# A transformer block on one core: head groups paired in one PSUM bank, merged causal masks, fewer waits, and a written list for each engine

## What is computed

```python
h = _layernorm(x) * (1 + ca) + sa
q, k, v = (split_heads(h @ W + b) for W, b in ((Wq, bq), (Wk, bk), (Wv, bv)))
att = softmax(where(causal, einsum('bhtd,bhsd->bhts', q, k) / sqrt(8), -inf))
y = einsum('bhts,bhsd->bhtd', att, v).transpose(...).reshape(B, T, 128) @ Wo + bo
x = x + ga * (layernorm(y) * gamma + beta)
h = _layernorm(x) * (1 + cb) + sb
x = x + gb * (sum over the top 2 experts of coef * ((silu(h @ gate) * (h @ up)) @ down)
              + (silu(h @ shared_gate) * (h @ shared_up)) @ shared_down)
```

## Time and profile before

| | us |
|---|---|
| Median of 3 runs (551.6 to 552.94) | 552.45 |
| The profiled execution | 553.16 |
| its span on the core | 551.4 |
| PE busy in the span | 502.8 (91%) |
| DVE, ACT, POOL busy | 359.7, 292.2, 254.1 |
| prologue, first turn | 0 to 24.9, 24.9 to 78.4 |
| middle turns | 78.4 to 446.9 |
| final turn, tail | 446.9 to 505.5, 505.5 to 551.4 |

### The profile page before, as it was taken

The page is one execution under the profiler, slowest core; times in us unless marked ns, Lnnn a source line. Parts: engine busy times, 40 slices in busy tenths (PEclk is TensorE's granted clock), DMA queues, the critical chain, the costliest instruction groups (busy, mean ns, idle before and its releaser), DMA issues.

```text
span 551.4 us, 10280 instructions
## 1 busy us (share of the span) xinstructions
PE 502.8 (91%) x3626; PEld 273.1 (50%) x3626; DVE 359.7 (65%) x806; ACT 292.2 (53%) x615; POOL 254.1 (46%) x366
## 2 busy tenths in 40 slices
...
DMA packets 35795, 37.93 MB, mean 69 GB/s; under 512 B 8832, under 2 KB 30880, under 8 KB 35616
## 3 DMA queue, kind: packets, MB, share of 16 engines
...
## 4 chain that ended last, share of the span: by engine, by line
PE 68%; DVE 16%; ACT 7%; DMA 5%; issue 2%; SPq 1%; POOL 0%; DVEq 0%; POOLq 0%; ACTq 0%
PE s_bank L1233 11%; PE pv_bank L1265 10%; PE s_bank L1251 9%; PE gate_bank L1337 7%; PE up_bank L1348 7%; PE gate_bank L1380 6%; DVE row_max L1046 6%; PE s_bank L1235 4%; PE misc L1184 4%; ACT probs L860 3%; PE misc L1215 2%; DVE stats_x L994 2%; DMA k_stack<-k_scr 2%; PE up_bank L1289 2%; DMA q_stack<-max_rows 2%
## 5 line engine op out<-in xcount | busy, mean ns | idle before, releaser
L1046 DVE TENSOR_REDUCE row_max<-s_bank 128x1 f32<-128x512 f32 (+3 forms) x352 | 212.4, 635 | 57.0 <-PE s_bank L1235 54.7
L860 ACT ACTIVATE probs<-s_bank 128x512 f32<-128x512 f32 x320 | 181.5, 597 | 71.8 <-PE s_bank L1251 67.6
L1233 PE MATMUL s_bank<-k_stack,q_stack 72*128 72x256 bf16 (+3 forms) x512 | 136.4, 315 | 16.7 <-DMA q_stack<-q_scr 7.8
L1251 PE MATMUL s_bank<-q_stack,k_stack 75*128 75x128 bf16 (+3 forms) x512 | 118.0, 307 | 10.1 <-ACT probs L860 6.3
L728 POOL TENSOR_SCALAR_AFFINE_SELECT probs<-probs 128x512 f32<-128x512 f32 (+1 forms) x96 | 75.4, 791 | 97.8 <-ACT probs L860 97.1
L1235 PE MATMUL s_bank<-causal,ident_bf 128*128 128x128 bf16 x512 | 101.0, 227 | 0.0
L1265 PE MATMUL pv_bank<-probs,v_aug 128*32 128x512 f32 (+3 forms) x1024 | 90.6, 449 | 0.4 <-POOL probs L728 0.3
L1233 PEld LDWEIGHTS s_bank<-k_stack,q_stack 72*128 72x128 bf16 x512 | 51.7, 101 | 71.6 <-DVE row_max L1046 44.4
L1251 PEld LDWEIGHTS s_bank<-q_stack,k_stack 75*128 75x128 bf16 x512 | 42.3, 100 | 58.9 <-ACT probs L860 24.5
L1235 PEld LDWEIGHTS s_bank<-causal,ident_bf 128*128 128x128 bf16 x512 | 52.0, 102 | 16.6 <-issue 7.8
L713 POOL TENSOR_TENSOR hidden<-hidden,coef_sb 128x512 f32<-128x512 f32 x28 | 35.6, 1272 | 22.2 <-ACT coef_sb L914 22.2
...
## 6 DMA issues: line engine op xcount, KB each, us to landing
...
```

What stands on the lines that cost most here:

```text
L860: nc.scalar.activation(dst, src, ACT.Exp, scale=SCALE).then_inc(exp_done, 1)
L1046: nc.vector.reduce_max(row_max[s % 2][:, 0, h:h + nh, qt], s1_bank[u % 2][:, 0:nh * w].rearrange("p (h k) -> p h k", h=nh), AX_X).then_inc ...
L1233: nc.tensor.matmul(dst[:, w * i:w * (i + 1)], q_stack[0:KROWS, h, P * qt:P * (qt + 1)], k_stack[0:KROWS, h, 0:w], start=True, stop=False)
L1251: final = nc.tensor.matmul(dst[:, at:at + w], k_stack[0:MROWS, hh, P * j:P * (j + 1)], q_stack[0:MROWS, hh, P * j:T], start=True, stop=True)
```

## The change

- **Two head groups in one bank.** The four `pv` blocks of an even group and of the odd one behind it add into the same `pv_bank`. The values' window of 32 columns starts 8 columns earlier for the odd group, so its values come out on the next 8 partitions; the column of ones stands at 16 (even heads' groups) or 17. `uev` and `o` run once for two groups: in stage 3 (`o.3`, groups 0 and 1) and in stage 1 of the next turn (`o.1`, groups 2 and 3). DVE takes one reciprocal of twice the size and does two multiplies.
- **Merged masks.** One mask matmul for each `s1` unit, with `causal` repeated for its heads and a strided output.
- **The zero matmul before `down` is left out**; the first `down` matmul of a bank starts the accumulation.
- **Waits that others imply are left out**: those for `const_done` after the first turn, for the scratch writes except at `q`, `mods_in` after turn 1, and some for gate, up and `misc`.
- **A written list for each engine**, `ORDER[plan][engine]`, in place of the tables. In the first, final and tail turns the lists hold the same tasks in the same order as before, without the `uev` and `o` that went. In the middle turns the order is new on all five engines.

```diff
@@ constants
+PAIR = 2
+ONES_AT = PAIR * DH
+PAIRS = G // PAIR
@@ ORDER, "middle"
-        "extra": [
-            {0: [("xin", "next"), ("wdb", "prev"), ("uev", ""), ("xs", "next")], 5: [("o", "")],
...
-        "s1": [[0, 1, 5, 9, 9, 12, 12, 15, 16, 18, 22],
...
+        "pe": ("s1.0.0 pv.0.1 s2.0.0 s1.0.1 s2.0.1 pv.0.2 s2.0.2 s1.0.2 s2.0.3 pv.0.3 s1.0.3 s2.0.4 s1.0.4 s2.0.5"
+              " s1.0.5 s2.0.6 s1.0.6 s2.0.7 s1.0.7 s2.0.8 s1.0.8 s1.0.9 s2.0.9 s1.0.10 xt s1.1.0 pv.0.0 s1.1.1 q"
+              " s1.1.2 s1.1.3 pv.1.1 max.0 s1.1.4 pv.1.2 s1.1.5 k s1.1.6 s1.1.7 pv.1.3 s2.1.0 s1.1.8 s1.1.9 s2.1.1"
+              " o.1 s2.1.2 s2.1.3 s1.1.10 s2.1.4 ot s1.2.0 s2.1.5 s1.2.1 s2.1.6 y s1.2.2 s1.2.3 max.1 s2.1.7 s2.1.8"
+              " s1.2.4 v s1.2.5 pv.1.0 s2.1.9 s1.2.6 s2.2.0 s1.2.7 pv.2.1 pv.2.2 s2.2.1 pv.2.3 s2.2.2 s1.2.8 s2.2.3"
+              " s2.2.4 s1.2.9 s2.2.5 s2.2.6 s1.2.10 s2.2.7 s1.3.0 pv.2.0 s2.2.8 s2.2.9 s1.3.1 s1.3.2 x2t pv.3.1"
+              " s1.3.3 g0 s1.3.4 lg s1.3.5 u0 g1 max.2 pv.3.2 s1.3.6 pv.3.3 s1.3.7 u1 o.3 s2.3.0 s2.3.1 s1.3.8 g2"
+              " s1.3.9 s2.3.2 s2.3.3 u2 ct s2.3.4 s2.3.5 g3 c0 s2.3.6 s1.3.10 s2.3.7 c1 u3 s2.3.8 g4 s2.3.9 u4 c2"
+              " pv.3.0 down0 c3 down1 down2 max.3 down3 down4"),
+        "dve": ("s1.0.0 xs s1.0.1 s1.0.2 s1.0.3 s1.0.4 s1.0.5 s1.0.6 s1.0.7 s1.0.8 s1.0.9 s1.0.10 s1.1.0 s1.1.1"
+              " s1.1.2 q s1.1.3 s1.1.4 s1.1.5 s1.1.6 s1.1.7 k s1.1.8 s1.1.9 o.1 s1.1.10 s1.2.0 s1.2.1 s1.2.2 s1.2.3"
+              " s1.2.4 s1.2.5 s1.2.6 yg s1.2.7 x2 x2stat s1.2.8 s1.2.9 s1.2.10 s1.3.0 x2n s1.3.1 s1.3.2 s1.3.3"
+              " s1.3.4 g0 route s1.3.5 prob u0 above s1.3.6 g1 s1.3.7 rank u1 o.3 g2 s1.3.8 s1.3.9 u2 s1.3.10 g3 u3"
+              " g4 u4 fin"),
+        "act": ("xin s2.0.0 s2.0.1 s2.0.2 s2.0.3 s2.0.4 s2.0.5 s2.0.6 s2.0.7 xt s2.0.8 s2.0.9 q max.0 k uev.1 s2.1.0"
+              " s2.1.1 s2.1.2 s2.1.3 s2.1.4 ot s2.1.5 s2.1.6 ystat max.1 s2.1.7 s2.1.8 v yn s2.1.9 s2.2.0 s2.2.1"
+              " s2.2.2 s2.2.3 s2.2.4 s2.2.5 s2.2.6 s2.2.7 s2.2.8 s2.2.9 x2t g0 route max.2 g1 uev.3 s2.3.0 s2.3.1 g2"
+              " s2.3.2 s2.3.3 ct s2.3.4 s2.3.5 c0 g3 s2.3.6 s2.3.7 c1 s2.3.8 g4 s2.3.9 c2 c3 max.3"),
+        "pool": ("wdb xs xn s2.0.3 s2.0.7 s2.0.9 msplit.0 ot q k s2.1.3 msplit.1 ystat s2.1.7 s2.1.9 s2.2.3 x2stat"
+              " s2.2.7 s2.2.9 msplit.2 rank s2.3.3 c0 s2.3.7 c1 c2 msplit.3 c3 s2.3.9"),
+        "sp": ("load.0 xres load.1 max.0 stack max.1 load.2 max.2 max.3 load.3 fin"),
@@ slots
-def slots(has_prev, has_cur, has_next, engine=None):
...
+def slots(has_prev, has_cur, has_next, engine="pe"):
+    plan = "first" if not has_prev else "tail" if not has_cur else "middle" if has_next else "final"
+    return [task(word) for word in ORDER[plan][engine].split()]
@@ waits: the pattern (inv_std, split_rest, xn, s2, ystat, rank, layer_stats, max)
-                need_written(pool, it)
-                need_all(pool, (const_done, 1), (misc_read, misc_at(it, name) + 1))
+                pool.wait_ge(misc_read, misc_at(it, name) + 1)
@@ part_first
-                need_written(act, it)
+                if name[1] == "q":
+                    need_written(act, it)
@@ uev
-                    act.wait_ge(pv_done, it * G + (s - 1))
-                    if not (isinstance(it, int) and (it, s) == (0, 2)):
-                        if s > 0:
-                            act.wait_ge(misc_written, misc_at(it, (s - 1, "o", 0)) + 1)
-                        else:
-                            act.wait_ge(misc_written, misc_at(it, misc_uses(it if isinstance(it, int) else 1)[0]))
+                    act.wait_ge(pv_done, it * PAIRS + s // PAIR)
@@ DVE, o
-                    g = (s - 2) % G
+                    r = 0 if s == PAIR + 1 else 1
                     dve.wait_ge(misc_written, misc_at(it, (s, "o", 0)) + 1)
-                    if g == 0 and not (isinstance(it, int) and it == 0):
-
-                        dve.wait_ge(misc_written, misc_at(it, (s_of(it, "ot"), "ot", 0)) + 1)
-                    view = misc[:, :].rearrange("p (c v) -> p c v", v=VC)
-                    nc.vector.reciprocal(denom[:, :].unsqueeze(2), view[:, :, DH:DH + 1]).then_inc(denom_ready, 1)
-                    dve.wait_ge(denom_ready, it * G + (s - 1))
-                    nc.vector.tensor_tensor(
-                        o_tok[:, :, GH * DH * g:GH * DH * (g + 1)].rearrange("p t (h d) -> p t h d", h=GH),
-                        misc[:, :].rearrange("p (t h v) -> p t h v", t=TT, h=GH)[:, :, :, 0:DH],
-                        denom[:, :].rearrange("p (t h) -> p t h", t=TT).unsqueeze(3).to_broadcast([P, TT, GH, DH]),
-                        ALU.mult).then_inc(misc_read, 1)
+                    view = misc[:, :].rearrange("p (t h v) -> p t h v", t=TT, h=GH)
+                    nc.vector.reciprocal(denom[:, :, :, :], view[:, :, :, ONES_AT:ONES_AT + PAIR]).then_inc(denom_ready, 1)
+                    dve.wait_ge(denom_ready, it * PAIRS + s // PAIR)
+                    for i in range(PAIR):
+                        g = PAIR * r + i
+                        final = nc.vector.tensor_tensor(
+                            o_tok[:, :, GROUP * g:GROUP * (g + 1)].rearrange("p t (h d) -> p t h d", h=GH),
+                            view[:, :, :, DH * i:DH * (i + 1)],
+                            denom[:, :, :, i:i + 1].to_broadcast([P, TT, GH, DH]), ALU.mult)
+                    final.then_inc(misc_read, 1)
@@ PE, s1
-                                         k_stack[0:KROWS, h, 0:w], start=True, stop=False)
-                        final = nc.tensor.matmul(dst[:, w * (i + 1) - P:w * (i + 1)], ident_bf[:, :], causal[:, :],
-                                                start=False, stop=True)
-                    final.then_inc(s1_written, 1)
+                                         k_stack[0:KROWS, h, 0:w], start=(i == 0), stop=False)
+                    diagonal = dst[:, 0:nh * w].rearrange("p (h k) -> p h k", h=nh)[:, :, w - P:w]
+                    nc.tensor.matmul(diagonal, ident_bf[:, :], causal[:, :].unsqueeze(1).to_broadcast([P, nh, P]),
+                                     start=False, stop=True).then_inc(s1_written, 1)
@@ PE, pv
-                        need(pe, u_ready, it * G + (s - 1))
-                        wait_v(pe, it - (s == 0), misc_read, v_read)
+                        if g % PAIR == 0:
+                            need(pe, u_ready, it * PAIRS + n // PAIR)
+                        if n == 0:
+                            wait_v(pe, it, misc_read, v_read)
+                    odd = g % PAIR
+                    values = v_aug[(it - (n < 0)) % 2][:, j, :, :].rearrange("p h v -> p (h v)")
                     for h in range(GH):
-                        final = nc.tensor.matmul(pv_bank[VC * h:VC * (h + 1), P * j:T], v_aug[(it - (n < 0)) % 2][:, j, GH * g + h, :],
+                        at = VC * (GH * g + h) - DH * odd
+                        final = nc.tensor.matmul(pv_bank[VC * h:VC * (h + 1), P * j:T], values[:, at:at + VC],
                                                 probs[g % 2][:, h, P_AT[j]:P_AT[j] + T - P * j],
-                                                start=(a == 0), stop=(a == len(PV_ORDER) - 1))
-                    if a == len(PV_ORDER) - 1:
+                                                start=(a == 0 and not odd), stop=(a == len(PV_ORDER) - 1 and odd == 1))
+                    if a == len(PV_ORDER) - 1 and odd:
@@ PE, max and o
-                    need_all(pe, (const_done, 1), (max_step, it * (G * 2) + 2 * (s + 1)), (misc_read, misc_at(it, (s, "max", 0))))
+                    pe.wait_ge(max_step, it * (G * 2) + 2 * (s + 1))
+                    take_misc(it, (s, "max", 0))
...
-                    pe.wait_ge(u_ready, it * G + (s - 1))
+                    pe.wait_ge(u_ready, it * PAIRS + s // PAIR)
@@ PE, down
-                        pe.wait_ge(gate_read, it * GATE_USES - 1)
                         pe.wait_ge(wd_ready, it)
                         if last(it):
                             pe.wait_ge(exp_done, it * (G * U2))
-                        for bank, w in ((s2_bank[0], T // 2), (s1_bank[0], T // 2)) if last(it) else ((gate_bank, T),):
-                            nc.tensor.matmul(bank[:, 0:w], zero_row[:, 0:P], zero_row[:, 0:w], start=True, stop=False)
                     elif last(it):
                         pe.wait_ge(coef_used, a)
                     else:
                         pe.wait_ge(weighted, it * FB + (a - FB))
                     for t in range(TT):
-                        last_mm = nc.tensor.matmul(down_of(it, t), hidden[:, m, P * t:P * (t + 1)], wd_b[:, m, :], start=False,
+                        last_mm = nc.tensor.matmul(down_of(it, t), hidden[:, m, P * t:P * (t + 1)], wd_b[:, m, :],
+                                                   start=(a == 0 and (t == 0 or (last(it) and t % 2 == 0))),
```

171 lines of the change are left out of this document (45 added, 126 removed), and 113 rows, old and new, of the table ORDER.

## The result

The changed kernel takes 542.97 us (median of four runs, 542.44 to 546.63) where the kernel before takes 552.09: a ratio of 0.985 (0.981 to 0.989), 9.1 us less. The forecast was 537.8 us with a range of 526 to 549. Sign and range hold; of the 14.6 us forecast 5.5 did not come, and the 9 that came are only in part those of the sum. The profiled execution took 542.44 us with a span of 540.7.

A forecast was written before the change was run, and what follows sets the result against it. A middle turn was TensorE's own 57.6 us of work plus 2.9 us of gaps. Six turns at -2.1 (-12.5), final turn -1.3, first turn -0.4 and tail -0.4 make -14.6, from 552.45 to 537.8 us; range 526 to 549.

The forecast's parts named there:

- The terms of work: TensorE's own work in a middle turn: `o` -0.88, masks -0.15, zero matmul -0.3, islands +0.66, together -0.67 us.
- The zero matmul: On TensorE before `down`: leaving it out saves 0.3 us a turn, since no other work fills that time.
- Masks: Merged masks on TensorE: 0.15 us a turn saved, between bounds of 0 and 1.2, because the columns stay.
- Islands: `pv` blocks split apart on TensorE in middle turns: three more islands at 0.22 us each, +0.66 us a turn.
- the gaps: TensorE's waits in a middle turn: 2.9 us before, 1.5 after, a gain of 1.4 us a turn.
- The single gaps: Expected middle-turn waits: stage 0 0.4; `max.0`, `ot`, `v`, stage 1 max rows 0.2 each; 0.3 for misses.
- still covered: Stages 2 and 3: TensorE's 8.4 us between `lg` and `ct` hides the chain from `x2t`, whose DVE and POOL steps sum to 7.0.
- Rival A: In middle turns the gaps only move and only work goes: 6.1 us less, 546.3 us; chance 0.20.
- Rival C: Maxima reach `q_stack` late before `s2`: a 4.0 us chain costs 3.0 a turn, 555.8 us; chance 0.13.
- Queues: Moved tasks on SP and POOL: SP's loads are in time; `ot` ahead of POOL's splits has about 1.5 us slack.
- Rival B: All gaps go, and with them turn 1's low clock, some 4 us: 525 us; chance 0.17.
- First turn, final turn, tail: Outside the middle turns: first turn -0.4 us, final turn -1.3, tail -0.4.

The follow-up runs named there:

- e12: e10's kernel with one mask for each head again, 16 in a stage instead of 11; middle turns 59.13 or 59.14 us, one execution of 535.2 us.
- e2: The changed kernel with the middle turns in the order of the kernel before, on all five lists; 60.06 us a turn, ratio 0.989.
- e6: e10's kernel with consumers moved back: `max.0` behind `pv.1.2`, `x2t` and `x2n` one unit earlier; turns 59.15 us, total 536.8 us, ratio 0.968.
- e9: e10's kernel with producers `q`, `q_rest` and `x2n` moved ahead, and `x2t`, `pv.3.2` and `max.2` reordered; 538.9 us, ratio 0.976.
- e8: e10's kernel with `pv.0.1`, `pv.0.2` and `pv.0.3` together again behind `s1.0.0`; middle turns 58.96 us, single execution 546.9 us.
- e3: The changed kernel with the last `max` transpose of a middle turn one `down` block earlier on TensorE; 539.6 us, ratio 0.976.
- e7: The changed kernel with the last `max` transpose of a middle turn one `down` block later on TensorE; some 547 us, ratio 0.991.
- e1: The changed kernel run again, unedited; 543.8 us, ratio 0.983 to the kernel before.
- e10: The changed kernel with the last `max` one `down` block earlier and `stack` behind the stage 1 max rows; 539.5 us, ratio 0.977.
- e11: e8's kernel run once more, beside e10; 541.0 us, ratio 0.981.

## Why the prediction was right or wrong

**The terms of work.** The zero matmul: 0.31 us (`down0` went from 1.309 to 0.995), forecast 0.3. Masks: 22 ns for a four-head unit and 8 to 9 ns for a two-head one, 0.155 us a turn, forecast 0.15, and e12 confirms it by itself. The low bound was the right one: columns cost, instructions hardly. `o`: two of 0.44 us. Islands: 0.09 in and about 0.09 out, 0.18 where I took 0.22; three of them 0.54 instead of 0.66. The rest of the fall in work, some 0.5 us, was not forecast and is in small pieces: `y` 1.28 to 1.11 us, `k`, `q`, gate and up 0.10 to 0.15 each. In all 56.3 us of work for 57.6, a fall of 1.3 against 0.67 forecast.

**The step that failed is the gaps**: still 2.9 us and not 1.5. It failed in two ways. First, I let the saved work come off while the old gaps stood. e2 shows that they don't stand: of 1.35 us of work 0.9 did not reach the turn. The gaps grew by 1.2: 0.6 in stage 0, where PE's partners kept the stage as long as it was (I had read one `o` on DVE there and overlooked the one at the head of the turn), 0.3 at `ot` behind the merged `o`, and 0.3 at `max.2` behind POOL's split, which I did not look at. Second, the new lists then earned what I said they would, 0.8 us for 0.7, but from 4.1 down. Taken apart, one turn: e2's step is work -1.65 and gaps +1.2, the lists' step work +0.35 and gaps -1.15; together -1.27 for the -2.1 forecast. The split between work and gaps is a reading of starts and good to some 0.1 to 0.2 us; the lengths are measured.

**The single gaps.** At `max.0` 0.54 for the 0.2 forecast: I took the 1.6 us from the end of `q` to the end of `q_rest` in a place where DVE was free. Now `q_rest` stands behind a reduction, 1.8 us, and the start of `max` follows 0.15 after it, which I had not counted; the cover is the 1.4 that I said. At `x2t` 0.50, not seen at all: "still covered" was said of a chain that I began at `x2t` and not at `x2n`. `ot` 0.13 and `v` none (0.2 forecast for each). Stage 0: 1.0 for 0.4, 0.26 of it the max rows. And ACT still releases three `s2` units late, by 0.14, 0.30 and 0.30, where I had taken its gaps (1.35) away.

**Rival A** (gaps only move) is what a middle turn shows, and e6 and e9 show it twice more: with 0.5 us or 1.0 us of named waits removed, turns took 59.15 and 58.99 us (in e9 0.3 of the gaps went, and work took their place). e8 is the same in reverse. It has its limit: e3's 0.26 and e12's 0.16 went through in full. The difference that the runs show is whether the wait was for a transfer, or the work was spread over the turn, or it was one of the waits tied to DVE. That is a pattern in these runs and not a tested rule: in e2 the same masks went together with `o` and the zero matmul, and which of the three was lost is open.

**Rival C** (the hand-over of the maxima) was held at 0.13 with 3.8 us as the point of decision. It happened in one place of four. At the end of a turn the chain, where PE waited for it, takes 3.2 to 3.6 us and not the 2.8 of the earlier trace rows:

```profile
254.26 0.24 PE L1166 MATMUL misc<-ident_bf,row_max 128*48 128x128 bf16 x1
...
257.77 0.39 PE L1139 MATMUL s_bank<-q_stack,k_stack 75*128 75x512 bf16 x1 [0.23 <-DMA q_stack<-max_rows]
```

e3 and e7 price it: near this point cover gained or lost shows in the turn, -0.27 and +0.73 us. In stage 1 the rows stood behind `stack` as I wrote, but I priced it at 0.2 us in every turn, and it was 0 in most and 0.8 to 1.4 in turn 4.

**Queues.** I walked SP and POOL for what moved, and missed a move that is in no list: `xin` keeps its place on ACT, but the task ahead of it, `max.3`, waits for a transpose that went one `down` block back, and the end of the turn, with one `o` less, comes sooner. That cost 3.9 us once (turn 5) and nothing in e1.

**Rival B.** Its second half came true: the low clock of turn 1 is gone, 3.9 us with what else that turn gained. I gave it no share in the forecast and charged the splitting of `pv`, which by e8, e10 and e11 keeps it away, with cost alone.

**First turn, final turn, tail.** Final -0.7 for -1.3. The forecast took the old gaps as standing in the final turn too. The -2.4 us of turn 0 and -2.5 of the tail for -0.4 each are mostly not the change's: over e1 to e8, whose first turns have the same lists, turn 0 took 51.0 to 58.2 us and the tail 43.8 to 48.7, by how long the clock was low. At equal low clock little is left: e10's turn 0 (29.0 us low) takes 53.1 for the 53.5 before (28.6 low), e1's tail 46.1 for 45.9 (17.1 low in both). So the sum came near partly by luck: of the 10.7 us in the profile, 4.8 lie in turns 1 to 6, for which 12.5 were forecast.
